# One chunk of layer 1 in two fp32r passes over stacked high and low rows

## The reference, cut to what matters

```python
e = jnp.stack([tbl_f[ids[:, f]] for f in range(39)], axis=1)     # 1024 x 39 x 16
x0 = xk = e
for W in (f0, f1, f2):                                           # three layers of 128 outputs
    z = jnp.einsum('bfd,bgd->bfgd', x0, xk).reshape(b, f * g, d)
    cur = jnp.einsum('bpd,pm->bmd', z, W)
    outs.append(cur); xk = cur
z = jnp.sum(jnp.concatenate(outs, axis=1), axis=-1)
h = jnp.concatenate([z, dense_ctx], axis=1)
h = jnp.maximum(h @ W_top1 + b_top1, 0.0)
h = jnp.maximum(h @ W_top2 + b_top2, 0.0)
y = h @ W_top3
```

## Time and profile before

| | us |
|---|---|
| median of 3 runs (1288.04 to 1289.68) | 1289.47 |
| the profiled execution, its own time | 1290.09 |
| its span, from the first to the last instruction | 1288.3 |
| TensorE (PE) busy | 1246.9 |
| VectorE (DVE) busy | 1039.1 |
| GpSimd (POOL) busy | 949.5 |
| ScalarE (ACT) busy | 749.3 |

### The profile page before, as it was taken

One profiled execution on the slowest core, in us unless ns is written; L12 is line 12 of the kernel. 1 busy time (PEld: TensorE's weight loads), 2 busy tenths in 40 slices (PEclk: granted clock), 3 DMA queues, 4 the chain that ended last, 5 costly groups with the idle time before them and its releaser, 6 DMA issues.

```text
span 1288.3 us, 19892 instructions
## 1 busy us (share of the span) xinstructions
PE 1246.9 (97%) x5493; PEld 964.5 (75%) x5493; DVE 1039.1 (81%) x3346; ACT 749.3 (58%) x2422; POOL 949.5 (74%) x844
## 2 busy tenths in 40 slices
PE   0799999999999999999999999999999999999999
PEld 0577778777787778777787777877787777877765
DVE  4679886889968997799878998699977999788840
ACT  4456665666646665566656666466655666466641
POOL 6568887788868887688867888588866888675640
PEclk9999999999999999999999999999999999999999
DMA  7632221122222212122211222222121222111000
GB/s 166 170 107 68 68 69 39 51 60 63 64 67 61 54 47 66 49 68 68 69 42 48 63 64 62 66 63 53 46 65 49 68 68 68 46 43 50 1 1 1
DMA packets 121764, 78.69 MB, mean 61 GB/s; under 512 B 77436, under 2 KB 89826, under 8 KB 121652
## 3 DMA queue, kind: packets, MB, share of 16 engines
q1 hardware_dynamic: 106124, 73.45, 20.2%
q0 software_dynamic: 10240, 2.64, 2.3%
q10 hardware_dynamic: 5288, 1.32, 0.5%
HBM read 18.50 MB, written 2.63 MB: 16 GB/s over the span
## 4 chain that ended last, share of the span: by engine, by line
PE 95%; DMA 2%; ACT 1%; SPq 1%; DVE 0%; issue 0%; ACTq 0%; DVEq 0%
PE ps L492 23%; PE ps L496 22%; PE ps L493 22%; PE ps L472 14%; PE ps L517 6%; PE ps L508 5%; PE ps L574 2%; PE ps L584 1%; DMA dense_rows<-in_dense_ctx 1%; DMA w<-in_f 1%; PE ps L455 1%; SPq L359 0%; ACT ps L699 0%; SPq L271 0%; PE ps L591 0%; ACT w_high L701 0%
## 5 line engine op out<-in xcount | busy, mean ns | idle before, releaser
L816 DVE SCALAR_TENSOR_TENSOR terms<-ps,x_scal,terms 128x128 f32<-128x128 f32 x2944 | 807.3, 344 | 162.1 <-ACT terms L661 94.3
L661 ACT ACTIVATE terms<-ps,x_scal 128x128 f32<-128x128 f32 x2048 | 583.5, 368 | 375.8 <-PE ps L496 368.8
L410 POOL TENSOR_TENSOR terms<-terms 128x1024 f32<-128x1024 f32 (+2 forms) x384 | 576.7, 1502 | 186.2 <-DVE terms L816 163.7
L492 PE MATMUL ps<-w_high,x_high 128*128 128x512 f32 (+1 forms) x1280 | 582.9, 455 | 6.4 <-DMA w<-in_f 4.9
L496 PE MATMUL ps<-w_high,x_low 128*128 128x512 f32 (+1 forms) x1280 | 496.7, 388 | 0.0
L493 PE MATMUL ps<-w_low,x_high 128*128 128x512 f32 (+1 forms) x1280 | 494.8, 387 | 0.0
L386 POOL DMA_INDIRECT x_in<-in_tables,row_at x320 | 304.2, 951 | 81.7 <-issue 67.3
L492 PEld LDWEIGHTS ps<-w_high,x_high 128*128 128x128 f32 x1280 | 241.0, 188 | 86.5 <-issue 18.5
L493 PEld LDWEIGHTS ps<-w_low,x_high 128*128 128x128 f32 x1280 | 241.6, 189 | 78.0 <-issue 29.8
L496 PEld LDWEIGHTS ps<-w_high,x_low 128*128 128x128 f32 x1280 | 240.5, 188 | 50.8
L472 PE MATMUL ps<-prods,w 117*128 117x512 f32 x262 | 134.6, 598 | 9.4 <-DVE prods L782 9.4
(11 more groups left out here) (48 smaller groups left out, 412.8 us busy)
## 6 DMA issues: line engine op xcount, KB each, us to landing
prods<-x_cols SPq DMA_DIRECT2D x190, 234.0 KB
x_cols<-x_rows SPq DMA_DIRECT2D x93, 78.0 KB
x_first<-x_cols SPq DMA_DIRECT2D x93, 78.0 KB
x_in<-in_tables,row_at POOLq DMA_INDIRECT x320, 2.4
x_diag<-x_scal SPq DMA_DIRECT2D x256, 9.8 KB
s<-in_f SPq DMA_DIRECT2D x3, 832.0 KB, 11.4
x_rows<-x_in SPq DMA_DIRECT2D x31, 80.0 KB, 2.4
wt<-in_W_top SPq DMA_DIRECT2D x1, 768.0 KB, 12.6
```

Source lines behind the costliest of these rows:

```text
L410: nc.gpsimd.tensor_tensor(t[:, 0:n], t[:, 0:n], t[:, n:2 * n], ALU.add).then_inc(s_tree, 1)
L492: nc.tensor.matmul(y, x1_high[:, par, at:at + P], high, start=True, stop=False)
L661: op = nc.scalar.activation(terms[:, u % 2, FB * ACT_BANKS.index(q) + i, :], ps[:, (BANKS * u + q) % RING, i * G:(i + 1) * G], ACT.Copy, s ...
L816: nc.vector.scalar_tensor_tensor(out=acc, in0=y, scalar=x0, in1=acc, op0=ALU.mult, op1=ALU.add).then_inc(s_mac, 1)
```

## The change

The chunk with two distances comes second in the order (`SHIFT_OF`). Its 78 product rows are split like those of other chunks, but into one tile `rest` of 117 rows: its rows 0 to 77 hold the high part, written by ScalarE, and its rows 78 to 116 hold 39 low rows at a time. VectorE writes all 78 low rows into `prods_low`, from where they are moved behind the high rows by a transfer, the first 39 by ScalarE's queue at (0, 8) and the second 39 by SP's queue once the first pass is done. The weights `w0_rest` are laid out to match: one version has high weights above the copied high weights of the first distance, the other has low weights above the copied high weights of the second distance. The chunk is made in two fp32r passes, at (1, 3) and (2, 1). The three-pass chunks are now 2, 3 and 4, and the chunks 0, 5 and 6 stay fp32. For the first group, which has no split, the chunk is one fp32 matmul in two halves of its columns.

`dense_rows` now lies in a part of `r2` that is not yet in use, which makes room for the new tiles.

```diff
-SPLIT = (1, 2, 3)
+SHIFT_OF = (0, KT - 1) + tuple(range(1, KT - 1))
+REST, SPLIT = 1, (2, 3, 4)
 NS = len(SPLIT)
+KH = (SPT - 1) * F
-PRODUCTS = ((0, 2), (0, 4), (1, 2), (1, 7), (2, 3), (2, 5), (2, 7))
-HIGHS = ((0, 6), (1, 4), (1, 8))
-LOWS = ((0, 7), (1, 5), (1, 9))
-CIN1 = ((0, 6), (1, 1), (1, 8), (2, 6), (2, 9), (3, 2), (3, 4))
+PRODUCTS = ((0, 2), (0, 4), (1, 2), (1, 7), (2, 1), (2, 5), (2, 7))
+HIGHS = ((0, 6), (1, 4), (1, 8), (2, 2))
+LOWS = ((0, 7), (1, 5), (1, 9), (2, 3))
+MOVE_LOWS = (0, 8)
+CIN1 = ((0, 6), (1, 3), (1, 8), (2, 1), (2, 6), (2, 9), (3, 2), (3, 4))
+CIN1_OF = (0, REST, 2, REST, 3, 4, 5, 6)
+SLOTS = len(CIN1)
+REST_SLOTS = tuple(n for n, k in enumerate(CIN1_OF) if k == REST)
...
+        rest = sb("rest", [KR, GCOLS], F32R)
+        w0_rest = sb("w0_rest", [KR, 2, G], F32R)
...
+        def move_rest(queue, i):
+
+            queue.dma_start(rest[KH:KR, :].bitcast(F32), prods_low[i * F:(i + 1) * F, 0, :].bitcast(F32)) \
+                .then_inc(s_rest, 16)
...
             def move_seconds(gf, j):
 
-                for k in range(1, KT):
-                    sp.wait_ge(s_cin1, gf * KT - KT + k + 1)
-                    move_second(sp, k, j)
+                for n in range(1, SLOTS):
+                    sp.wait_ge(s_cin1, gf * SLOTS - SLOTS + n + 1)
+                    if n == REST_SLOTS[0] and gf > 1:
+                        move_rest(sp, 1)
+                    if n != REST_SLOTS[0 if gf == 1 else 1]:
+                        move_second(sp, CIN1_OF[n], j)
...
                 move_diag(gf, j)
                 if more:
                     move_seconds(gf + 1, j + 1)
+                else:
+                    sp.wait_ge(s_cin1, gf * SLOTS + REST_SLOTS[0] + 1)
+                    move_rest(sp, 1)
...
             next_cols(1, 1)
+            sp.wait_ge(s_w0l, 1)
+            for i in range(2):
+                sp.dma_start(w0_rest[KH:KR, i, :].bitcast(F32), w0_rest[i * F:(i + 1) * F, 0, :].bitcast(F32)) \
+                    .then_inc(s_wrest, 16)
             move_seconds(1, 1)
...
-            def cin1(gf, k, first=False):
-
+            def cin1(gf, n, first=False):
+
+                k, half = CIN1_OF[n], REST_SLOTS.index(n) if n in REST_SLOTS else 0
+                cols = slice(0, GCOLS)
...
+                elif k == REST:
+                    pe.wait_ge(s_wrest, 32)
+                    pe.wait_ge(s_rest, (gf - 1) * 32 + half * 16 + 16)
+                    passes = ((w0_rest[:, half, :], rest[:, :]),)
...
-                act.wait_ge(s_prod, gf * KT + SPLIT[i] + 1)
-                nc.scalar.activation(prods_high[:, i, :], prods[0:KR, SPLIT[i], :], ACT.Copy).then_inc(s_high, 1)
+                k = ((REST,) + SPLIT)[i]
+                act.wait_ge(s_prod, gf * KT + k + 1)
+                if k == REST:
+                    act.wait_ge(s_cin1, (gf - 1) * SLOTS + REST_SLOTS[1] + 1)
+                    nc.scalar.activation(rest[0:KH, :], prods[0:KH, k, :], ACT.Copy).then_inc(s_high, 1)
+                else:
+                    nc.scalar.activation(prods_high[:, i - 1, :], prods[0:KR, k, :], ACT.Copy).then_inc(s_high, 1)
...
+                    if front and (tile, q) == MOVE_LOWS:
+                        act.wait_ge(s_low, (gf - 1) * (NS + 1) + 1)
+                        move_rest(act, 0)
...
             def split_low(gf, i):
 
-                dve.wait_ge(s_high, gf * NS - NS + i + 1)
-                nc.vector.tensor_tensor(prods_low[:, i, :], prods[0:KR, SPLIT[i], :],
-                                        prods_high[:, i, :].bitcast(F32), ALU.subtract).then_inc(s_low, 1)
+                dve.wait_ge(s_high, (gf - 1) * (NS + 1) + i + 1)
+                k = ((REST,) + SPLIT)[i]
+                if k == REST:
+                    if gf > 1:
+                        dve.wait_ge(s_cin1, (gf - 2) * SLOTS + SLOTS + CIN1_OF.index(SPLIT[-1]) + 1)
+                    nc.vector.tensor_tensor(prods_low[0:KH, 0, :], prods[0:KH, k, :],
+                                            rest[0:KH, :].bitcast(F32), ALU.subtract).then_inc(s_low, 1)
+                else:
+                    if i == NS:
+                        dve.wait_ge(s_rest, gf * 32)
+                    nc.vector.tensor_tensor(prods_low[:, i % NS, :], prods[0:KR, k, :],
+                                            prods_high[:, i - 1, :].bitcast(F32), ALU.subtract).then_inc(s_low, 1)
```

More of the change, by code:

```diff
@@ L114, in pair_rows @@
     k, i, f = np.ogrid[:KT, :SPT, :F]
+    k = np.array(SHIFT_OF)[k]
     g, h = (f - KT * i) % F, (f + k) % F
@@ L163, in cin_tower @@
         bt2 = sb("bt2", [P, H2 // P])
-        dense_rows = sb("dense_rows", [P, NBATCH, ROWS3])
         dense_t = sb("dense_t", [ROWS3, B], F32R)
@@ L169, in cin_tower @@
         w0_a, w0_b = (terms_flat[0:KR, i * KT * G:(i + 1) * KT * G] for i in range(2))
+        dense_rows = r2[:, 0:NBATCH * ROWS3].rearrange("p (c k) -> p c k", k=ROWS3)
         h1 = terms_flat[:, 0:2 * H1 // P * 512].rearrange("p (h c n) -> p h c n", h=2, c=H1 // P)
@@ L199, in cin_tower @@
         s_prod = sem("products_ready")
+        s_rest = sem("rest_lows_moved")
+        s_wrest = sem("w0_rest_moved")
         s_high = sem("product_highs_ready")
@@ L270, in move_second @@
             at = j % GROUPS * GCOLS
-            queue.dma_start(prods[0:KR, k, :], x0_cols[k:k + KR, at:at + GCOLS]).then_inc(s_second[k - 1], 16)
+            row, n = SHIFT_OF[k], KH if k == REST else KR
+            queue.dma_start(prods[0:n, k, :], x0_cols[row:row + n, at:at + GCOLS]).then_inc(s_second[k - 1], 16)
+        def move_rest(queue, i):
+            queue.dma_start(rest[KH:KR, :].bitcast(F32), prods_low[i * F:(i + 1) * F, 0, :].bitcast(F32)) \
+                .then_inc(s_rest, 16)
         def prologue_then_batches(eng, step, prologue, tail):
@@ L457, in turn_scalars @@
                 mm.then_inc(s_st, 1)
-            def cin1(gf, k, first=False):
+            def cin1(gf, n, first=False):
+                k, half = CIN1_OF[n], REST_SLOTS.index(n) if n in REST_SLOTS else 0
+                cols = slice(0, GCOLS)
                 if k == 0:
                     pe.wait_ge(s_scal, gf + 1)
-                if k in SPLIT and not first:
+                if k == REST and first:
+                    pe.wait_ge(s_prod, k + 1)
+                    cols = slice(half * 256, half * 256 + 256)
+                    passes = ((w0[0:KH, k, :], prods[0:KH, k, cols]),)
+                elif k == REST:
+                    pe.wait_ge(s_wrest, 32)
+                    pe.wait_ge(s_rest, (gf - 1) * 32 + half * 16 + 16)
+                    passes = ((w0_rest[:, half, :], rest[:, :]),)
+                elif k in SPLIT and not first:
                     i = SPLIT.index(k)
-                    pe.wait_ge(s_low, gf * NS - NS + i + 1)
+                    pe.wait_ge(s_low, (gf - 1) * (NS + 1) + i + 2)
+                    low = prods_low[:, (i + 1) % NS, :]
                     passes = ((w0_high[:, i, :], prods_high[:, i, :]), (w0_low[:, i, :], prods_high[:, i, :]),
-                              (w0_high[:, i, :], prods_low[:, i, :]))
+                              (w0_high[:, i, :], low))
                 else:
@@ L470, in cin1 @@
                     passes = ((w0[:, k, :], prods[0:KR, k, :]),)
-                for n, (w, x) in enumerate(passes):
-                    mm = nc.tensor.matmul(ps[:, X1_BANK, :], w, x, start=(k == 0 and n == 0),
-                                          stop=(k == KT - 1 and n == len(passes) - 1))
+                for i, (w, x) in enumerate(passes):
+                    mm = nc.tensor.matmul(ps[:, X1_BANK, cols], w, x, start=(k == 0 and i == 0),
+                                          stop=(n == SLOTS - 1 and i == len(passes) - 1))
                 mm.then_inc(s_cin1, 1)
@@ L535, in prologue @@
                 pe.wait_ge(s_denl, len(DENSE_BANKS))
[L536 to L539, removed]
+                for n in range(SLOTS):
+                    cin1(0, n, True)
+                pe.wait_ge(s_w0h, NS + 1)
+                pe.wait_ge(s_w0l, NS + 1)
                 pe.wait_ge(s_w1h, len(W1_PIECES))
@@ L642, in split_high @@
             def split_high(gf, i):
-                act.wait_ge(s_prod, gf * KT + SPLIT[i] + 1)
-                nc.scalar.activation(prods_high[:, i, :], prods[0:KR, SPLIT[i], :], ACT.Copy).then_inc(s_high, 1)
+                k = ((REST,) + SPLIT)[i]
[5 more added lines that the diff above has]
+                    nc.scalar.activation(prods_high[:, i - 1, :], prods[0:KR, k, :], ACT.Copy).then_inc(s_high, 1)
             def store_x1(gf, j):
-                act.wait_ge(s_cin1, gf * KT + KT)
+                act.wait_ge(s_cin1, gf * SLOTS + SLOTS)
                 nc.scalar.activation(x1_high[:, j % 2, :], ps[:, X1_BANK, :], ACT.Copy).then_inc(s_x1h, 1)
@@ L691, in prologue @@
                 act.wait_ge(s_w0s, 1)
+                nc.scalar.activation(w0_rest[0:KH, 0, :], w0[0:KH, REST, :], ACT.Copy).then_inc(s_w0h, 1)
                 for i, k in enumerate(SPLIT):
```

(15 more changed lines are left out.)

## The result

The changed kernel takes 1566.78 us (median of 4 runs, 1560.71 to 1567.39) against 1289.58 us before: a ratio of 1.2138, with an interval of 1.2104 to 1.2172. It is slower, by 277 us, and lies inside the range. The profiled execution took 1567.39 us, 27.8 us more than the 1539.6 of the sum.

What follows compares the result with a forecast made beforehand. TensorE, busy 97% of the span, was taken as the bound. Plain windows +228.4, first +18.3, closing -1, last +3.3 and prologue +0.5 sum to 249.5 over 1290.09, so 1539.6, forecast 1539 us, range 1480 to 1600.

Steps and rivals of the forecast that it cites:

- the sum: All windows and prologue together: 249.5 us added to the profiled 1290.09 us, giving 1539.6 us.
- The place of the move: SP's queue issues the second half's move behind the diagonal moves, 25.36 us into a plain window; TensorE wants it at 18.37.
- plain windows: 22 spans between layer 2 tile starts, building a layer 1 group without closing a batch: 35.29 to 45.67 us, +228.4 total.
- the chain's start: SP's first step per window, storing gathered rows, stays 12.0 us into the window despite the stall.
- The transfer: The second half's move takes 2.1 us from issue to landing, with ends 1.6 and 3.1.
- The clock: TensorE idles about 9 us per plain window, then runs at 1.2 GHz, losing 1.7 us a stall, ends 0 and 3.4.
- closing windows: Seven windows where layer 3's passes close a batch in tile 1; second pass nearly in time, -1 us in all.
- The other windows: Beside the plain ones: first window +18.3 us, seven closing ones -1 in all, last +3.3; prologue +0.5.
- What lies beside: First half's move, extra splits on ScalarE and VectorE: no cost, even without the stall's cover; prologue +0.5 us.
- the first rival: SP issues the second half's move in time, keeping the 12.4 us saving less the prologue: 1277 us; chance 5%.
- A sign that did not come: In the profile after, TensorE's busy time for layer 1 would fall; no size given.
- The rule on issuing early and waiting late: Issue a transfer early, wait late, so fixed cost overlaps; by slots (1, 3) to (2, 1), this gives 1277 us; 5%.

Runs made afterwards that it cites:

- experiments 1 to 3: Changed kernel with the second half's move issued by ScalarE (1291.74 us), as SP's first step (1295.38 us), or ahead of the diagonal moves only (1426.67 us).
- experiment 4: Changed kernel with extra matmuls ahead of the second pass, 36 in each plain window and 64 in the first: 1521.27 us.
- experiment 1: Changed kernel with the second half's move issued by ScalarE at (1, 3) instead of by SP: 1291.74 us.
- experiment 7: On experiment 1, with chunks 5 and 6's products later and copied weight rows moved by ScalarE: chunk 2's product from (1, 2) to (1, 1); 1283.67 us.
- experiment 8: On experiment 7: fourth low split to (2, 7), chunk 4's passes to (3, 0), chunk 5's product back to (2, 5); 1280.12 us.

## Why the prediction was right, point by point

**The place of the move** was the step on which everything rested, and it held: the rest move left 25.20 us into the plain windows on average (25.36 was forecast), the chain's start stayed at 12 us, and experiments 1 to 3 show that the stall is as long as the move is late.

**The transfer** was mis-sized: 2.60 us from issue to the start of the second pass instead of 2.1. I had ended it with the last bytes of the earlier trace rows. Those bytes were not late: in the trace of the kernel after, over the plain windows, the move's last packet ends 2.0 us behind its issue on average. Then the last step of its semaphore comes at 2.46 and the pass at 2.60, so the missing 0.5 lies between the last bytes and TensorE's start. Over 22 windows it is 11 us. The Trainium skill's page "DMA: Bandwidth & Descriptors" (Anatomy of one DMA — SWDGE (gpsimd) path) fits 2.0 us plus bytes / 436e3 to transfers that GpSimd issues. Taken over to this one, which SP issues, it would give an estimate of 2.0 us and 0.18 for 78 KB, 2.2: also short of the measured time.

**The clock** was right in kind and too small: from the second pass to the window's end it took 18.81 us where 18.21 were forecast with a loss of 1.7. Against the 16.70 of experiment 4 the loss is 2.1, against the closing windows' 16.55, which lose nothing, 2.3; over 22 windows 9 to 13 us more than forecast. The two waits of the earlier trace rows were too few to give a mean. With the chain's -3.5 these two terms make up most of the 27.8.

**The other windows.** The first came out at +18.9 and a prologue of +1.4, forecast 18.3 and 0.5. The closing ones were forecast within -0.3 to +0.1 and rose by 0.26. Each waits 0.5 for ScalarE's store, which I had not seen. The store starts 15.2 us into a closing window before and in experiment 1 alike; with 0.47 us less TensorE work ahead in tile 1 it is now the later of the two, and in experiment 7, with ScalarE earlier, the wait is gone. The last rose by 5.7 instead of 3.3, since its 3.2 us of waiting cost it the clock in full: from the second pass to its end it took 19.3 us, and 16.9 in experiment 1.

**What lies beside** holds only half. Under the stall the additional splits cost nothing, as forecast, and the first half's move was never late in a plain window. But I wrote that without that cover they would cost nothing either, as long as VectorE and ScalarE wait for TensorE, and gave the first rival 1277 us. That step failed: with the move in time the kernel is at 1291.74, not 1277. VectorE does wait for TensorE at the end of tile 3, but not in tile 2; there the fourth split, lengthened by GpSimd's additions, held a bank back, and 13 of 22 plain windows lost 0.3 to 0.5 us by it, as much as the change saves. The rest of the 12.4 went into the closing windows (+0.1 each instead of -0.4) and the first (+2.7, in which the wait for layer 3's weights rose from 4.9 to 6.9 us, and +1.1 ahead of it).

**A sign that did not come.** The wait's line, the place of the move, the chain's start and the fall of the clock in every plain window came as forecast, but TensorE's busy time for layer 1 did not fall. Over the whole span it is 214.5 us for L472 before and 217.6 for L510 after, mostly since 24 of the second passes stand right behind a wait, at 1.2 GHz, and last 0.76 us instead of 0.40.

**The rule on issuing early and waiting late**, from the Trainium skill's page "DMA: Bandwidth & Descriptors" (Rules for kernel authors), which I had weighed as a rival, is not contradicted; the change followed it by slots alone. In these runs the place in the queue decided when the transfer was issued.

## What to carry to other kernels

A transfer that one engine waits for was here as late as the last thing ahead of it in the queue that issued it, whatever its own condition said: before a wait is added, read in the trace where that queue stands at that moment. An idle time of another engine counts as cover only if it lies in the same stretch as the added work, and the added work's length has to be taken from a moment at which the same neighbours run. A small saving on a full engine is kept only if the engines that free its buffers are earlier by as much; in experiment 8, with the split and the store earlier or out of the way, the plain windows keep 0.31 of the 0.40 us.

## What the runs showed of the hardware that was not expected

A low split of VectorE that takes about 0.68 us takes 1.57 to 1.60 when an addition of GpSimd in SBUF has just begun, for it ends 0.55 us behind that addition; an addition that begins during the split does not lengthen it (experiment 1). Whether that costs TensorE anything hung on 0.4 us in its start or length. Of the 2.60 us from the rest move's issue to the pass, 0.6 come after the last packet. Filling a wait of 9 us with matmuls whose results nobody reads made this kernel 46 us faster than leaving TensorE idle (experiment 4), since the clock then stayed at 2.4 GHz.
